# Two attentions of a four-layer transformer kernel: value matmuls in four bursts an item instead of one row a round

## The reference, cut to what matters

```python
x = x + ln(L0_attn(ln(x)))    # 16 heads of 8, scores clipped to +-10: no maxima wanted
x = x + ln(L0_ffn(ln(x)))     # holds a latent attention (16 heads, scores over 48 numbers), then experts
x = x + ln(L1_attn(ln(x)))    # 16 heads of 8, true softmax
x = x + ln(L1_ffn(ln(x)))
# each attention, causal, x of shape (4, 1024, 128):
att = softmax(where(mask, q @ k.T * scale, -inf))
y = att @ v
```

## Time and profile before

| | us |
|---|---|
| median of 3 executions | 1923.18 (1916.9 to 1938.81) |
| span of the profiled execution | 1941.8 |
| PE busy | 1696.7 (87%) |
| DVE busy | 1296.8 (67%) |
| ACT busy | 1143.6 (59%) |
| POOL busy | 661.8 (34%) |
| value matmuls (L992), all three attentions | 462.7 busy |

### The profile page before, as it was taken

The page is one execution under the profiler, slowest core; times in us unless marked ns, Lnnn a source line. Parts: engine busy times, 40 slices in busy tenths (PEclk is TensorE's granted clock), DMA queues, the critical chain, the costliest instruction groups (busy, mean ns, idle before and its releaser), DMA issues. The chain is left out here.

```text
span 1941.8 us, 38672 instructions
## 1 busy us (share of the span) xinstructions
PE 1696.7 (87%) x13334; PEld 704.4 (36%) x13334; DVE 1296.8 (67%) x2458; ACT 1143.6 (59%) x1788; POOL 661.8 (34%) x1227
## 2 busy tenths in 40 slices
PE   6878878597899999999999888886699999999886
PEld 4311212243343433434333555454333333333232
DVE  6677778574766666666662346665478888888254
ACT  6789999442055555555556433334327777777746
POOL 6465565575232222312222001104312222222464
PEclk9799999798899999999999998998659999999998
DMA  8533335168212312313210410001502222222201
GB/s 241 126 66 60 54 68 142 32 153 175 40 40 40 67 51 51 67 41 67 50 41 23 142 43 1 0 1 49 171 21 49 48 49 48 46 47 68 45 28 44
DMA packets 91800, 125.99 MB, mean 65 GB/s; under 512 B 24501, under 2 KB 63797, under 8 KB 91398
## 3 DMA queue, kind: packets, MB, share of 16 engines
q1 hardware_dynamic: 89526, 121.17, 27.2%
q10 hardware_dynamic: 2096, 2.47, 0.4%
HBM read 75.90 MB, written 47.58 MB: 64 GB/s over the span
## 5 line engine op out<-in xcount | busy, mean ns | idle before, releaser
L1059 ACT ACTIVATE q_buf<-ps 128x1024 f32<-128x1024 f32 (+1 forms) x1152 | 864.1, 822 | 453.3 <-PE ps L935 450.4
L1171 DVE TENSOR_REDUCE o_sb<-ps 128x1 f32<-128x512 f32 (+3 forms) x864 | 712.5, 865 | 248.1 <-PE ps L970 163.1
L1124 POOL TENSOR_SCALAR_AFFINE_SELECT q_buf<-q_buf 128x256 f32<-128x256 f32 x768 | 364.5, 499 | 768.6 <-ACT q_buf L1059 637.4
L992 PE MATMUL ps<-q_buf,v_buf 128*9 128x512 f32 (+7 forms) x4608 | 462.7, 497 | 59.8 <-POOL q_buf L1124 55.2
L935 PE MATMUL ps<-q_buf,k_buf 49*128 49x512 f32 (+3 forms) x1536 | 320.3, 518 | 0.0
L935 PE MATMUL ps<-q_buf 48*128 48x512 bf16 (+7 forms) x1536 | 261.8, 334 | 33.6 <-ACT q_buf L1059 26.7
L1231 DVE TENSOR_SCALAR q_buf<-q_buf 128x1024 f32<-128x1024 f32 x288 | 218.0, 765 | 57.1 <-ACT q_buf L1059 53.3
L992 PEld LDWEIGHTS ps<-q_buf,v_buf 128*9 128x9 f32 (+1 forms) x4608 | 95.1, 96 | 237.6 <-issue 118.2
L935 PEld LDWEIGHTS ps<-q_buf 48*128 48x128 bf16 (+1 forms) x1536 | 75.4, 94 | 283.7 <-ACT q_buf L1059 225.8
L935 PEld LDWEIGHTS ps<-q_buf,k_buf 49*128 49x128 f32 x1536 | 131.5, 188 | 125.8 <-ACT q_buf L1059 53.7
L456 PE MATMUL ps<-w_wg,identity 128*128 128x512 f32 (+1 forms) x214 | 108.6, 633 | 31.0 <-PEq L113 31.0
(11 more groups left out here) (183 smaller groups left out, 1565.8 us busy)
## 6 DMA issues: line engine op xcount, KB each, us to landing
q_buf<-qm_d SPq DMA_DIRECT2D x32, 384.0 KB, 6.5
qm_d<-pr_buf SPq DMA_DIRECT2D x80, 128.0 KB, 2.4
o_d<-pr_buf SPq DMA_DIRECT2D x16, 512.0 KB, 2.7
q_buf<-o_d SPq DMA_DIRECT2D x8, 1024.0 KB, 5.1
q_d<-q_buf SPq DMA_DIRECT2D x48, 128.0 KB, 2.1
k_d<-q_buf SPq DMA_DIRECT2D x48, 128.0 KB, 1.9
k_buf<-km_d SPq DMA_DIRECT2D x32, 192.0 KB, 6.6
q_buf<-q_d SPq DMA_DIRECT2D x60, 96.0 KB
```

The source lines that it names most:

```text
L992: mm = nc.tensor.matmul(ps[VW * j:VW * j + V_ROWS_OUT, o_bank + half % O_BUFS, lo * P:(lo + nq) * P], v, units(i, r, j)[:, 0, off * P:(off ...
L1059: nc.scalar.activation(units(i, g, WIDE * e, WIDE), ps[:, bank:bank + WIDE, :], ACT.Exp, scale=scale).then_inc(s_e, 1)
L1124: nc.gpsimd.affine_select(out=blk, in_=blk, compare_op=ALU.is_ge, fill=0.0, base=0, pattern=[[0, 2], [1, P]], channel_multiplier=-1)\
L1171: nc.vector.tensor_reduce(to, sc, AX_X, ALU.max).then_inc(s_mr, 1)
```

## The change

In am and a1 a round no longer ends with one value row. Round 4 ends with rows 0, 1 and 2, round 6 with rows 3 and 4, round 8 with rows 5 and 6, and round 1 of the next item with rows 7 and 8. Rounds 0, 2, 3, 5 and 7 have none. Since row 0 now waits until round 4, the ring holds six rows of probabilities, not four; the two new rows lie in a free part of the large buffer (am) or in `pr_buf` (a1). What is computed, and each matmul, exponential, mask and reduction, stays. a0 keeps its ring of four and one value row a round. ACT's copies stay after the first exponential of rounds 2 and 5.

```diff
-            PLAG, PRING = 2, 4
+            PRING = 6 if has_max else 4
+            VALUES = {4: (0, 1, 2), 6: (3, 4), 8: (5, 6), 1: (-2, -1)} if has_max else \
+                {g: (g - 2,) for g in range(ROWS_P)}
...
             ring = area[:, 16384:24576].rearrange("p (u t) -> p u t", t=UNIT)
-
-            def units(i, g, j, cnt=1):
-
-                at = ((ROWS_P * i + g) % PRING) * QUAD + j
-                return ring[:, at:at + cnt, :]
+            ring_more = area[:, 12288:16384].rearrange("p (u t) -> p u t", t=UNIT) if latent else pr_buf[:, 0:8, :]
+
+            def units(n, g, j, cnt=1):
+
+                row = (ROWS_P * n + g) % PRING
+                at = (row % 4) * QUAD + j
+                return (ring if row < 4 else ring_more)[:, at:at + cnt, :]
...
-                            if g >= PLAG:
-                                value_row(n, i, g - PLAG)
-                            elif last != 0:
-                                value_row(n - 1, i - 1, g - PLAG + ROWS_P)
+                            for r in VALUES.get(g, ()):
+                                if r >= 0:
+                                    value_row(n, i, r)
+                                elif last != 0:
+                                    value_row(n - 1, i - 1, r + ROWS_P)
```

More of the change, by code:

```diff
@@ L702, in attention @@
             REDUCES = UNITS // M_WIDE
-            assert NQ % PRING == 0
             o_bank, s_bank0, m_bank0 = 0, O_BUFS, O_BUFS + WIDE * NSB
@@ L993, in value_row @@
                                     ps[VW * j:VW * j + V_ROWS_OUT, o_bank + half % O_BUFS, lo * P:(lo + nq) * P], v,
-                                    units(i, r, j)[:, 0, off * P:(off + nq) * P],
+                                    units(n, r, j)[:, 0, off * P:(off + nq) * P],
                                     start=(k == 0), stop=(g in (A_ROWS - 1, ROWS_P - 1)), tile_position=(0, VW * j),
@@ L1028, in item @@
                                     max_pair(n, b, i, *ahead, done // 2 - 1)
-                            if g >= PLAG:
-                                value_row(n, i, g - PLAG)
-                            elif last != 0:
-                                value_row(n - 1, i - 1, g - PLAG + ROWS_P)
+                            for r in VALUES.get(g, ()):
[3 more added lines that the diff above has]
+                                    value_row(n - 1, i - 1, r + ROWS_P)
                     def rest():
-                        for g in range(ROWS_P - PLAG, ROWS_P):
+                        for g in range(ROWS_P - 2, ROWS_P):
                             value_row(ITEMS - 1, ITEMS - 1, g)
@@ L1058, in item @@
                                     act.wait_ge(s_pv, ROWS_P * n + g + 1 + (g - PRING == A_ROWS - 1) + BASE)
-                                nc.scalar.activation(units(i, g, WIDE * e, WIDE), ps[:, bank:bank + WIDE, :],
+                                nc.scalar.activation(units(n, g, WIDE * e, WIDE), ps[:, bank:bank + WIDE, :],
                                                      ACT.Exp, scale=scale).then_inc(s_e, 1)
                                 if has_max and e == 0:
-                                    if g == PLAG and last != 0:
+                                    if g == 2 and last != 0:
                                         copy_output(b, i - 1, 1)
-                                    if g == A_ROWS + PLAG:
+                                    if g == A_ROWS + 2:
                                         copy_output(b, i, 0)
@@ L1122, in item @@
                                 for off in DIAG[g]:
-                                    blk = units(i, g, 2 * p, 2)[:, :, off * P:(off + 1) * P]
+                                    blk = units(n, g, 2 * p, 2)[:, :, off * P:(off + 1) * P]
                                     nc.gpsimd.affine_select(out=blk, in_=blk, compare_op=ALU.is_ge, fill=0.0, base=0,
@@ L1228, in item @@
                                 for p in range(2):
-                                    two = units(i, g, 2 * p, 2)
+                                    two = units(n, g, 2 * p, 2)
                                     dve.wait_ge(s_e, EXPS * n + 2 * g + p + 1 + NSB + BASE)
@@ L1233, in item @@
                                                             ALU.max, ALU.min).then_inc(s_clip, 1)
-                                    if p == 0 and g == PLAG and last != 0:
+                                    if p == 0 and g == 2 and last != 0:
                                         copy_output(b, i - 1, 1)
-                                    if p == 0 and g == A_ROWS + PLAG:
+                                    if p == 0 and g == A_ROWS + 2:
                                         copy_output(b, i, 0)
```

## The result

The changed kernel is slower: 2010.6 us median (2007.5 to 2021.6) against 1930.6 for the kernel before in the same series, a ratio of 1.0446 with a 95% interval of 1.0387 to 1.0505. That is 80 us where 7 were forecast, and outside the range. Its profiled execution has a span of 2005.7 us.

A forecast was written before the change was run, and what follows sets the result against it. It took PE to bound am and a loop through ACT's exponentials to bound a1. Terms: -10 (am) + 14 + 2 (a1) + 1 (clock) = +7 us on 1923, so 1930 us, range 1908 to 1952.

The forecast's parts named there:

- am: In am, fewer tile changes less DVE's waits save 0.63 us an item, 10 us in all.
- Rival 1: In am and a1, each change of tile removed is gain: -56, 1867 us; chance 0.13.
- a1's copies: In a1's rounds 2 and 5, now without values, ACT is the bound and each copy costs 0.48 us, 0.96 an item.
- a1 with the clock held: a1's item goes from 25.08 to 25.93 us, losing 14 us in all, plus 2 us for DVE.
- The clock: At a1's start the clock's rise may come later, 0 to 3 us; 1 us taken.
- rival 4: In a1 the clock falls in rounds without values: 1.9 us an item, 30 in 16 items, 1960 us; chance 0.14.
- The range: Whole kernel from 1908 us, leaving out rival 1, to 1952, leaving out half of rival 4.
- The rise of the clock at the start of a1: In a1's item 0 the rise comes with the first value row, now two rounds later; 1 us taken.

The follow-up runs named there:

- am_only: Kernel before with the bursts and the ring of six in am alone, a1 as before: 1916.0 against 1926.0 us, ratio 0.9951.
- again: Changed kernel with the maxima matmuls run twice in a1's rounds without values: 1960.2 us against 1926.0 for the kernel before, ratio 1.0156.
- again_copies: Changed kernel with a1's maxima matmuls doubled in rounds without values and ACT's copies moved to rounds 4 and 6: 1949.9 against 1925.6 us before.
- lone_again: am with bursts, a1 as before with one value row a round, its maxima matmuls doubled in rounds 0, 2, 3, 5, 7: 1930.4 against 1928.9 us before.
- ring6: Kernel before with the ring of six in am and a1, value rows still one a round: 1927.9 against 1926.0 us.
- mid: am with bursts; a1 with one value row a round, moved between third and fourth score units, copies after rounds 1 and 4's last exponential: 1904.8 against 1925.6 us before.

## Why the prediction was wrong, step by step

- **am: right.** Forecast -0.63 us an item and -10 in all; measured -0.60 and -10 ("am_only"). Its mechanism shows too. Pairs of maxima over the end of round 5 were forecast 1.33 apart:

```profile
582.79 0.39 PE L963 MATMUL ps<-k_buf,q_buf 48*128 48x512 bf16 x2
583.01 1.04 PE L939 MATMUL ps<-q_buf,k_buf 49*128 49x512 f32 x4
584.13 0.39 PE L963 MATMUL ps<-k_buf,q_buf 48*128 48x512 bf16 x2
```

  They are 1.34 apart: DVE's wait took back most of the 0.35 us of tile changes. Rival 1, that every change of tile removed is gain, falls with it.
- **a1's copies: right in kind, priced twice too high.** Forecast 0.96 an item; 0.44 between the items at full clock of "again" and "again_copies". These were taken with filler in the same rounds; without it the price was not seen apart from the clock.
- **a1 with the clock held: right in its total, partly by luck.** Forecast +0.85 and 0.1 for DVE, so 26.0 an item; by "again" less "lone_again" (27.14 - 26.17) +0.97, so 26.05. But the copies, the main term of that sum, gave 0.44, and the other 0.5 was not taken apart. The changed kernel itself never ran a1 at full clock. Its item less half of its low time (30.72 - 5.1) gives 25.6, an estimate that takes every low microsecond for half a lost one.
- **The clock: the step that failed.** The sum had 1 us for it, at the start of a1 only. The text gave the drop in rounds without values as rival 4, with 0.14, and set against it that nothing of the kind showed in 350 us of a1 and that "bursts keep the mean load nearly the same". The mean load did stay (PE busy 331 and 329 us of 350) and told nothing, the less so as matmuls at the lower clock count as busy for twice as long. What the change does is to make rounds without values; the clock fell behind these, and "again", which put work into them and nothing else, took the drops away in nearly every item. That shows the cause.
- **The price of rival 4 was mis-sized as well**: 1.9 us an item, with rounds 2 and 3 slow and 1 us of the burst. Measured, the drop comes after rounds 2 and 3, lies over round 4 and all of the burst (2.03 us lost there alone), and a second one lies behind round 5: 10.2 us low an item, of which 4.7 lost (30.72 - 26.05). With that the parts add up, as an estimate: -10 for am, 16 x 0.97 = 16 for the bursts and 16 x 4.7 = 75 for the drops, 81 together, where 80 were measured.
- **The range** did not hold either: it left out the cases in which the clock drops in every item, the ones that came.
- **The rise of the clock at the start of a1, 1 us of the sum, was read into one profile.** The prediction took it to come with the first value row, though with a doubt. In the changed kernel's profile the clock is at 1.00 from before 1390 until it drops at about 1419, and the first value matmul of a1 comes only at 1425.0, so the rise does not need one. Nor does it come whenever PE is busy: in the profile of before PE was busy all of 50 us and the clock stayed at 0.50. Before, then changed:

```profile
1390.00:1440.00 50.00, 50.00 (x201) 18.44 (x201) 32.43 (x32) 0.00 (x0) 0.91 (x4) 0.50 0.19 36
...
1390.00:1400.00 10.00, 9.79 (x77) 4.28 (x76) 10.00 (x10) 0.00 (x0) 0.00 (x0) 1.00 0.01 1
```

  Why one profile rose early and the other late stays open. The 16 us between the two at that place are not the change's doing: from am's last mark to a1's second it is 416 us in the profile of before and 400 in that of the changed kernel, but 402 in "ring6", which has the order of before.

By one rule of the Trainium skill ("TensorE: Matmul & The Clock Gate", section "HAM oscillation — how this bites in real kernels"), the clock falls when PE is left idle in one long gap. This case's trace differs: the gaps of PE ahead of the drops were under 0.4 us, and PE was busy 90% and 78% of the 4.6 and 3.4 us before them.

## What to carry to other kernels

When work is regrouped and its sum stays the same, look at the lightest stretch that the new order makes, not at the mean: here one or two rounds in a row without their dense matmuls brought TensorE down to 1.2 GHz, and the dense burst behind them then ran at half speed. Look at what work is left there, not at PE's busy share alone: "mid" kept its clock through a stretch with 77%, with value matmuls in it. Before gathering small waits on TensorE into one burst, ask which engine is the bound in the rounds left over; an ACT copy of 0.5 us that was free in a full round cost about half its time in an empty one, and moving the two away took two thirds of the low clock with them. Try such a change stage by stage: the same edit gained 10 us in the stage that TensorE bounds and lost 87 in the one bound by a loop through ACT.

## What the runs showed of the hardware

- With more matmuls (3647 instead of 2905 in 350 us) the clock stayed at 1.00 in nearly every item and the kernel got 50 us faster: repeating work was cheaper than leaving TensorE light.
- The drops locked to the loop: the items of the changed a1 were 30.72 us long to within 0.02, one after another, each with 6.8 and 3.4 us at the lower clock.
- PE's busy share did not tell the clock by itself: 78% of 3.4 us ahead of a drop in the changed kernel, 77% of 3.4 us with no drop in "mid", and 100% of 50 us at 0.50 at the start of a1 in the profile of before.
- Columns streamed at nearly the speed that either level gives: 1280 fp32 columns in 4.30 us at 1.2 GHz and 2.27 at 2.4 GHz.
